# Attention normalised in its transposed layout, with its sums sent over DRAM, rotary partners swapped by DMA, and a new table of positions

## The reference

```python
xn = _layernorm(x)
x = x + _L0_attn_ref(xn, ...) + _L0_ffn_ref(xn, ...)
# plain attention: 16 heads of 8 channels
attn = exp_x / (sum(exp_x) + 1e-6)          # exp_x = exp(clip(scores - max, -50, 50))
out = (attn @ v) @ Wout.T
# second block: the same attention with rotary q and k
r = [x1 * cos - x2 * sin, x1 * sin + x2 * cos]   # neighbours x1, x2 of a head
x = rmsnorm(src + softmax(q k / sqrt(8)) v Wo)
shared = swiglu(x @ W_shared_in) @ W_shared_out
routed = sum over 8 experts of (h @ W2[e]) * w[:, e]   # two experts of a row have w > 0
out = rmsnorm(x + shared + routed)
```

## Time and profile before

| what | value |
|---|---|
| median of three runs | 2111.24 us (2108.23 to 2111.75) |
| the profiled execution | 2110.22 us, span 2108.4 us |
| mean granted TensorE clock | 0.993 |
| busy: PE, DVE, ACT, POOL | 1957.9, 1629.0, 1442.8, 1135.9 us |
| DMA: moved, mean rate | 81.93 MB, 39 GB/s |

### The profile page before, as it was taken

The page is one execution under the profiler, slowest core; times in us unless marked ns, Lnnn a source line. Parts: engine busy times, 40 slices in busy tenths (PEclk is TensorE's granted clock), DMA queues, the critical chain, the costliest instruction groups (busy, mean ns, idle before and its releaser), DMA issues.

```text
span 2108.4 us, 43905 instructions
## 1 busy us (share of the span) xinstructions
PE 1957.9 (93%) x10694; PEld 602.4 (29%) x10694; DVE 1629.0 (77%) x2948; ACT 1442.8 (68%) x2993; POOL 1135.9 (54%) x1695
## 2 busy tenths in 40 slices
PE   4998899999999999999999999999999999999885
PEld 1222223232332323233232323323232222323232
DVE  3878897878879787887978788797978879797421
ACT  0367677777777777777777777777777777777752
POOL 1352637456473746647374664737466473746434
PEclk9999999999999999999999999999999999999997
DMA  2101010101101010110101010010101001010000
GB/s 92 43 27 50 28 53 31 56 27 53 36 24 56 29 57 26 52 36 25 56 28 58 26 55 32 26 56 27 59 26 54 31 27 56 26 56 18 22 0 16
DMA packets 79167, 81.93 MB, mean 39 GB/s; under 512 B 14716, under 2 KB 66172, under 8 KB 78844
## 3 DMA queue, kind: packets, MB, share of 16 engines
q1 hardware_dynamic: 78984, 80.20, 11.2%
HBM read 11.36 MB, written 4.19 MB: 7 GB/s over the span
## 4 chain that ended last, share of the span: by engine, by line
PE 71%; DVE 12%; issue 7%; ACT 6%; POOL 2%; SPq 1%; DVEq 1%; ACTq 0%; DMA 0%; POOLq 0%
PE o_ps L501 19%; PE score_ps L467 19%; PE side_ps L580 10%; DVE negmax L757 7%; PE side_ps L567 6%; PE shift_ps L482 5%; PE side_ps L549 5%; PE side_ps L516 3%; ACT weights L614 3%; DVE x L785 2%; PE side_ps L553 2%; PE side_ps L538 2%; PE side_ps L572 1%; ACT spread L649 1%; DVE stats L846 1%
## 5 line engine op out<-in xcount | busy, mean ns | idle before, releaser
L757 DVE TENSOR_REDUCE negmax<-score_ps 128x1 f32<-128x512 f32 x2048 | 1308.4, 682 | 350.0 <-PE score_ps L467 326.4
L614 ACT ACTIVATE weights<-shift_ps 128x512 f32<-128x512 f32 x2048 | 1161.2, 599 | 517.9 <-PE shift_ps L482 491.1
L482 PE MATMUL shift_ps<-qt,kt 51*128 51x512 bf16 x2048 | 691.3, 387 | 46.7 <-ACT weights L614 42.3
L467 PE MATMUL score_ps<-kt,qt 48*128 48x512 bf16 x2048 | 658.1, 393 | 58.6 <-DVE negmax L757 32.3
L954 POOL TENSOR_SCALAR weights<-weights 128x2048 f32<-128x2048 f32 x256 | 485.1, 1895 | 138.5 <-ACT weights L614 109.8
L501 PE MATMUL o_ps<-weights,vt 128*32 128x512 f32 x4096 | 550.1, 610 | 0.3 <-POOL weights L954 0.3
L467 PEld LDWEIGHTS score_ps<-kt,qt 48*128 48x128 bf16 x2048 | 131.7, 94 | 683.7 <-DVE negmax L757 544.6
L580 PE MATMUL side_ps<-w_sb,hidden 128*128 128x512 f32 x512 | 252.2, 617 | 9.9 <-ACT spread L649 8.1
L482 PEld LDWEIGHTS shift_ps<-qt,kt 51*128 51x128 bf16 x2048 | 150.4, 93 | 220.7 <-ACT weights L614 210.5
L649 ACT ACTIVATE spread<-side_ps,gate 128x128 f32<-128x128 f32 x512 | 159.8, 377 | 26.3 <-PE side_ps L580 26.3
L567 PE MATMUL side_ps<-x1T,w_up_sb 128*128 128x512 f32 x256 | 148.2, 665 | 6.3 <-DVE hidden L817 4.7
(11 more groups left out here) (111 smaller groups left out, 1452.0 us busy)
## 6 DMA issues: line engine op xcount, KB each, us to landing
qt<-q_parts SPq DMA_DIRECT2D x768, 32.0 KB
kt<-k_parts SPq DMA_DIRECT2D x768, 32.0 KB
x_in<-in_x_dram SPq DMA_DIRECT2D x16, 256.0 KB, 2.7
xn_mid<-xn_new SPq DMA_DIRECT2D x16, 256.0 KB, 2.4
xn_old<-xn_mid SPq DMA_DIRECT2D x16, 256.0 KB, 2.4
res_new<-in_x_dram SPq DMA_DIRECT2D x16, 256.0 KB, 2.6
res_old<-res_new SPq DMA_DIRECT2D x16, 256.0 KB, 2.7
out_dram<-out_sb SPq DMA_DIRECT2D x16, 256.0 KB, 2.6
```

The lines of the kernel that those rows point to most:

```text
L467: pe.matmul(score_ps[:, score_bank(a, t), :], qt[a][row:row + HROWS, slot, 128 * tile:128 * tile + 128], kt[a][row:row + HROWS, slot, :], ...
L482: pe.matmul(shift_ps[:, t % 2, :], kt[a][row:row + HROWS + MROWS, slot, 128 * tile:128 * tile + 128], qt[a][row:row + HROWS + MROWS, slot, ...
L614: act.activation(weights[:, i % 8, tile, :], shift_ps[:, t % 2, :], ACT.Exp, scale=SCALE).then_inc(weighed, 1)
L757: dve.tensor_reduce(negmax[:, i // 8, tile, i % 8:i % 8 + 1], score_ps[:, score_bank(a, t), :], AX.X, ALU.max, negate=True).then_inc(max_t ...
```

## The change

- **Normalisation in the transposed layout.** The jobs `o_*` and `back_*`, `normalise` and the copies into `headsT` go. `copy_o` still copies `o_ps` into `o_sb`; SP stores `o_sb` (256 KB) in DRAM (`move_o`), waits for it, and reads back the sums as `den` [128, 2, 32] and the channels as `heads_raw`. VectorE inverts `den` (`invert`, quarter 27 of each half); SP stores the inverses and, after that landed, reads them back repeated over the eight channels (`widen`) as `inv_wide`; GpSimd multiplies (`divide`) into `headsT`. `y_*` waits for that and stands at quarter 41 instead of 31.
- **Rotary partners by DMA.** `qs_rope` and `ks_rope` go. Channels are reordered on the chip so that partners lie 64 partitions apart (six ScalarE copies of the weights at the start). VectorE makes both products from one bank, two DMAs swap the halves of the sin product (`swing`), GpSimd adds it (`turn`). `q_rope` and `k_rope` move into the odd half before. cos and sin are loaded in four broadcast DMAs. `place_qk` reads every fourth partition instead of 32 neighbours.
- **Clips.** Every fourth head's clip goes from GpSimd to VectorE, as two instructions of 128x1024 with the lower bound alone; GpSimd keeps twelve.
- **Tables.** VALUE_AT is 3 instead of 1; all positions in EVEN and ODD are new (shared_out moves to the even half); banks are emptied one to two quarters later than before; the four row-tile pieces of the scalings, statistics and normalisation on VectorE, which stood together, are one per quarter or per two quarters.

The core of the diff; the remaining lines are the new positions on ScalarE and VectorE, semaphores and tiles:

```diff
+VALUE_AT = 3
...
+EVEN = [("v0", [1]), ("x1T", [3]), ("v1", [5]), ("gates", [9]), ("max_rope1", [11]), ("up0", [13]), ("down0", [17]),
+        ("up1", [21]), ("down1", [25]), ("up2", [29]), ("down2", [33]), ("up3", [37]), ("y_plain", [41]),
+        ("max_plain0", [43]), ("down3", [45]), ("shared_out", [53])]
+ODD = [("xnT", [1]), ("q_plain", [5]), ("max_plain1", [7]), ("k_plain", [9]), ("exp0", [13]),
+       ("exp1", [17]), ("exp2", [21]), ("exp3", [25]), ("exp4", [29]), ("exp5", [33]), ("exp6", [37]), ("y_rope", [41]),
+       ("max_rope0", [43]), ("exp7", [45]), ("q_rope", [53]), ("k_rope", [57])]
...
+AT = {"merge": 40, "invert": 27, "hi0": 7, "hi1": 9, "mid0": 13, "mid1": 17, "copy1": 21, "copy0": 53, "z": 33, "shares": 34, "top": 28,
+      "square_x1": 46, "scale_x1": 55, "square_out": 6, "scale_out": 13, "stats": 44, "moments": 51, "norm": 59}
...
                         sp.dma_start(kt[a][row:row + 8, 4 * gh:4 * gh + 4, :],
-                                     k_parts[a][p:p + 32, K_PART[t], :]).then_inc(qk_landed[a][gh], 16)
+                                     k_parts[a][c:128:4, K_PART[t], :]).then_inc(qk_landed[a][gh], 16)
 
             def place_max(b, job):
...
+            def move_o(b, job):
+
+                lag, a, gh = O_LAG[job], int(job[2:-1] == "rope"), int(job[-1])
+                if live(b, lag):
+                    hold(o_copied, cnt(b, lag, 4, 2 * a + gh + 1))
+                    if gh == 0:
+                        hold(normed, cnt(b, lag, 2, a))
+                    hold(den_moved, cnt(b, lag, 64, 16 * (2 * a + gh)))
+                    hold(rows_moved, cnt(b, lag, 64, 16 * (2 * a + gh)))
+                    sp.dma_start(o_rows, o_sb[:]).then_inc(o_out, 16)
+                    hold(o_out, cnt(b, lag, 64, 16 * (2 * a + gh + 1)))
+                    by_head = o_rows.rearrange("(r c) n -> r c n", c=16)
+                    sp.dma_start(den[:, gh, :], by_head[:, DH, :].rearrange("r (p n) -> r p n", n=DEN)).then_inc(den_moved, 16)
+                    sp.dma_start(heads_raw[64 * gh:64 * gh + 64, :], by_head[:, 0:DH, :]).then_inc(rows_moved, 16)
+
+            def widen(b, a):
+
+                if live(b, -1):
+                    hold(inv_done, cnt(b, -1, 2, a + 1))
+                    hold(inv_back, cnt(b, -1, 32, 16 * a))
+                    sp.dma_start(inv_rows.rearrange("(g h) (p n) -> (h p) g n", g=2, n=DEN), inv_den[:])\
+                        .then_inc(inv_out, 16)
+                    hold(inv_out, cnt(b, -1, 32, 16 * (a + 1)))
+                    hold(normed, cnt(b, -1, 2, a))
+                    sp.dma_start(inv_wide[:], inv_rows.unsqueeze(1).broadcast_to([H, DH, S]))\
+                        .then_inc(inv_back, 16)
+
+            def swing(b, n):
+
+                if live(b, 1):
+                    taken(sp, b, ("q_rope", "k_rope")[n])
+                    stand(sp)
+                    hold(rope_done, cnt(b, 1, 2, 0))
+                    for d0 in range(2):
+                        sp.dma_start(swung[64 * d0:64 * d0 + 64, n, :],
+                                     turned[64 * (1 - d0):64 * (1 - d0) + 64, n, :]).then_inc(swung_landed[n], 16)
...
                 place_max(b, "max_rope1")
+                move_o(b, "o_plain1")
...
+                widen(b, PLAIN)
                 place_qk(b, 0, ROPE, 0)
                 place_max(b, "max_plain0")
+                move_o(b, "o_rope0")
 
             def odd(b):
                 place_qk(b, 0, ROPE, 1)
                 place_max(b, "max_plain1")
+                move_o(b, "o_rope1")
+                widen(b, ROPE)
                 place_qk(b, 1, PLAIN, 0)
                 place_max(b, "max_rope0")
+                move_o(b, "o_plain0")
+                swing(b, 0)
+                swing(b, 1)
...
-                        pe.wait_ge(clip_pool, cnt(b, lag, H, 4 * quad + 4))
+                        pe.wait_ge(clip_pool, cnt(b, lag, 12, 3 * quad + 3))
+                        pe.wait_ge(clip_dve, cnt(b, lag, 8, 2 * quad + 2))
...
-                            if t == after("odd", f"exp{n}", 1 + half):
+                            if t == after("odd", f"exp{n}", 2 + 2 * half):
...
+            def clip(b, i, part):
+
+                if live(b, 0):
+                    dve.wait_ge(weighed, cnt(b, 0, 2 * UNIT, NT * i + 2 * part + 2))
+                    half = weights[:, i % 8, 2 * part:2 * part + 2]
+                    dve.tensor_scalar(half, half, FLOOR, None, ALU.max).then_inc(clip_dve, 1)
+
+            def invert(b, a):
+
+                if live(b, -1):
+                    dve.wait_ge(den_moved, cnt(b, -1, 64, 32 * (a + 1)))
+                    need(dve, inv_out, cnt(b, -1, 32, 16 * a))
+                    if a == PLAIN:
+                        dve.tensor_scalar(den[:], den[:], EPS_DEN, None, ALU.add).then_inc(den_done, 1)
+                        dve.wait_ge(den_done, cnt(b, -1, 1, 1))
+                    dve.reciprocal(inv_den[:], den[:]).then_inc(inv_done, 1)
...
+                    if (t - AT["scale_x1"]) % 2 == 0:
+                        scale(b, x1, x1, 0, -1, x1_done, (t - AT["scale_x1"]) // 2)
+                    for n, job in enumerate(("q_rope", "k_rope")):
+                        if t == after("odd", job) and live(b, 1):
+                            full(dve, b, job)
+                            need(dve, rope_rest, cnt(b, 1, 2, 0))
+                            need(dve, swung_landed[n], cnt(b, 1, 32, 0))
+                            dve.tensor_tensor(roped[:, n, :], bank(job), cos, ALU.mult)
+                            dve.tensor_tensor(turned[:, n, :], bank(job), sin, ALU.mult).then_inc(free(job), 1)
+
...
+            def turn(b, n):
 
                 if live(b, 0):
-                    taken(pool, b, ("q_rope", "k_rope")[n])
-                    taken(pool, b, last)
-                    pool.tensor_tensor(roped[:, n, :], roped[:, n, :], turned[:, :], ALU.add).then_inc(rope_done, 1)
+                    pool.wait_ge(swung_landed[n], cnt(b, 0, 32, 32))
+                    stand(pool)
+                    pool.tensor_tensor(roped[:, n, :], roped[:, n, :], swung[:, n, :], ALU.add).then_inc(rope_done, 1)
+
+            def divide(b, a):
+
+                if live(b, -1):
+                    pool.wait_ge(inv_back, cnt(b, -1, 32, 16 * (a + 1)))
+                    pool.wait_ge(rows_moved, cnt(b, -1, 64, 32 * (a + 1)))
+                    y = (b + (-1), "y_rope") if a == PLAIN else (b, "y_plain")
+                    if live(y[0], LAG[y[1]]):
+                        full(pool, *y)
+                    pool.tensor_tensor(headsT[:, :], heads_raw[:, :], inv_wide[:, :], ALU.mult).then_inc(normed, 1)
...
             def even(b):
-                clip(b + (-1), 15)
+                turn(b, 0)
+                turn(b, 1)
...
-                split_max(b, "max_plain0")
                 if live(b, -2):
                     router(b, True)
+                divide(b, PLAIN)
+                split_max(b, "max_plain0")
                 if live(b, 1):
```

More of the change, by code:

```diff
@@ L243, in layer_kernel @@
         ones_made = sem("ones_made")
+        wq_made = sem("wq_made")
         kt_ones = sem("kt_ones")
@@ L599, in step @@
                         side(b, job)
-            all_steps(pe, lambda b: step(b, "even"), lambda b: step(b, "odd"), merge_weights)
+            all_steps(pe, lambda b: step(b, "even"), lambda b: step(b, "odd"))
         @block.scalar
@@ L677, in even @@
                         copy_side(b, "x1T", x1T[:, :])
[L678 removed]
+                    if t == after("even", "max_rope1", 2):
                         copy_max(b, "max_rope1")
[L680 to L681 removed]
+                    part(b, 0, t, "q_rope", AT["hi0"], ROPE, roped[:, 0, :], q_parts, True)
+                    part(b, 0, t, "k_rope", AT["hi1"], ROPE, roped[:, 1, :], k_parts, True)
                     for n in range(4):
[L683 removed]
+                        if t == after("even", f"up{n}", 3) and live(b, -2):
                             full(act, b, f"up{n}")
@@ L804, in even @@
                                           ALU.add).then_inc(free("gates"), 1)
-                    for job, dst, table in (("q_rope", roped[:, 0, :], cos), ("qs_rope", turned[:, :], sin),
-                                            ("k_rope", roped[:, 1, :], cos), ("ks_rope", turned[:, :], sin)):
-                        if t == after("even", job) and live(b, 0):
-                            full(dve, b, job)
-                            need(dve, rope_rest, cnt(b, 0, 2, 0))
-                            if job == "ks_rope":
-                                dve.wait_ge(rope_done, cnt(b, 0, 2, 1))
-                            dve.tensor_tensor(dst, bank(job), table, ALU.mult).then_inc(free(job), 1)
                     for n in range(4):
-                        if t == after("even", f"up{n}", 2) and live(b, -2):
+                        if t == after("even", f"up{n}", 3) and live(b, -2):
                             dve.wait_ge(tanh_done, cnt(b, -2, 4, n + 1))
```

(13 more changed lines are left out.)

257 lines of the change are left out of this document (123 added, 134 removed), and 3 rows, old and new, of the table EVEN.

## The result

The changed kernel takes 2204.04 us (median of 4, 2193.28 to 2205.54) against 2110.26 (median of 4) for the kernel before beside it: 1.0434 times the time, 95% interval 1.0404 to 1.0464. I had forecast 2068 and a range of 2012 to 2138: wrong in sign and outside the range. The profiled execution of the changed kernel took 2193.28 us, its span is 2191.5, so 83.1 us longer than the span before.

The account below looks back on a forecast made before the run. PE and DVE together were taken to hold the even half, PE the odd. 57.5 + 62.0 = 119.5 against 122.6 a batch, over fifteen steps -45, last batch +2: 2110.2 to 2067, 2068 by the median; range 2012 to 2138.

Parts of the forecast that it names:

- the wait at y_plain: Even half, quarter 41: headsT comes 2.9 us after PE is ready; no fall of TensorE's clock priced behind it.
- the chain of flights: Even half, SP's queue: o's store, moves, inverses out and back, then GpSimd's product; headsT ready at 907.0.
- o's copy: Even half: ACT copies o at quarter 21, at 0.82 us a quarter about 888, starting the way over DRAM.
- Rival 2: Even half: y_plain's wait grows 1.8 us and halves TensorE's clock, +3; batch 124.3, total 2138 us; chance 0.22.
- the turn: Odd quarters 49 to 64, into the even half: 16.0 us of DVE work against 11 of PE, then 1.2 given back.
- three scalings: Odd quarters 49 to 64, on DVE: three x1 scalings at their median 0.61, 1.8 us together.
- odd quarters 0 to 13: Start of the odd half, without shared_out: 10.8 us, scaled from today's 16.1 us for 17 quarters.
- quarters 13 to 49 of the odd half: Stretch with all eight experts, y and a max: 36.4 us, with DVE's clips, inversion and additions fitting beside it.
- DVE's wait of 2 us for den: Even half, quarter 27: DVE reaches invert at 890.6, den lands at 893.2, so DVE stands 2 us or so.
- The tail: Last batch: the way over DRAM has only experts beside it; +2 us taken (0 to 12).
- The even half without the stall: Forecast for the even half: 57.5 us, ending at about 925.9, with the wait of 2.9 in it.
- rival 1: Whole loop: PE's full saving of 6.5 us per batch arrives, y_plain finds headsT ready; 2014 us; chance 0.18.

Follow-up runs that it names:

- e2_rope: Against the changed kernel: q_rope and k_rope at odd quarters 13 and 15 instead of 53 and 57, exp0 to exp7 one slot later; 2187.75 us.
- e4_fill: Against the changed kernel: PE multiplies three unused 128x512 f32 blocks ahead of y_plain's wait for headsT in the even half; 2171.34 us.
- e1_widen: Against the changed kernel: SP's even half issues inv_rows and inv_wide right behind xn_old's move, ahead of the other moves; 2129.92 us.
- f3_all: Against the changed kernel: earlier inverses, q_rope/k_rope, max_rope1 splitting, y_rope divide and q_plain parts; DVE's hidden product one quarter later; 2065.15 us.

## Why the prediction was wrong

**The step that failed** is the wait at y_plain: "Against it: I work out a wait of 2.9, for which no row shows a fall". The place, its cause in SP's queue and the chain of flights were right: 2.05 + 2.94 + 5.12 + 2.19 + 3.01 + 1.26 us were measured where I had 2.6, 2.63, 5.13, 2.6, 2.6 and 1.26 (2.94 and 5.12 from issue to issue, as 2.63 and 5.13 were). One term agrees by luck: o's copy "at quarter 21" would be at 868.4 + 21 x 0.82 = 885.6 and not 888, but the half starts slower than that pace, and the store left 19.4 us into it, close to what I wrote. The wait was 3.40 in the batch shown and 3.8 in the mean. The size hardly matters, because the clock also fell behind waits of 2.96 and, in e2_rope, 2.67: the wait of 2.9 that I worked out would have been no defence. One fall behind 4.71 shows that such a wait is enough; it says nothing of shorter ones, and I priced the clock behind mine at nothing. e4_fill prices it at 33 us and e1_widen the whole place at 74. Rival 2, which I gave 0.22 and let begin at 4.7, is what happened in the even half; its 2138 is still 66 short, and it holds nothing of the turn.

**The second step that failed** is the turn: "Fifteen maxima 9.3, two clips 2.4, four rotary products 2.5, three scalings at their median 0.61 1.8: 16.0", and then 1.2 given back. Quarters 49 to 64 took 18.6, of which 1.2 is DVE's wait at the jump, and the even half starts 2.0 later on top. The two clips there were cheaper than I had them (1.9 and not 2.4). The scalings are the term that was mis-sized: four of them stand there, at quarters 55, 57, 59 and 61, and not three, and they took 4.3 in the mean of eleven batches against my 1.8. Two of the four end right behind GpSimd's clips: 1.27 and 1.63 us in the turn shown, where a scaling takes 1.01 in the mean of all 64. The 1.2 that I gave back did not come. The groups after (xcount | busy us, mean ns | idle before):

```profile
L834 DVE TENSOR_SCALAR weights<-weights 128x1024 f32<-128x1024 f32 x128 | 99.8, 781 | 0.0
L856 DVE SCALAR_TENSOR_TENSOR x<-x,rms,norm_sb 128x128 f32<-128x128 f32 x64 | 64.2, 1007 | 1.6 <-POOL rms L1021 1.6
```

I took the median of a quantity whose long values belong to just this place, and priced DVE as a sum where the clock falls beside it as well; what that fall costs no run shows.

**What I did not look at:** the tables also move tanh and hidden into one quarter. DVE stood 0.46 us in front of each of four products, in a stretch where DVE had become the bound. And k_plain waits for the bank that q_plain's rest frees, 19.7 us in the whole kernel, 1.2 a batch, which is most of why odd quarters 0 to 13 take 12.3 and not 10.8 (11.3 in f3_all, where the first parts of q_plain come sooner). Its row on the page after:

```profile
L615 PE MATMUL side_ps<-xnT,wq_sb 128*128 128x512 f32 x96 | 58.7, 696 | 21.1 <-DVE q_rest L940 19.7
```

**What held:** quarters 13 to 49 of the odd half at 36.4 (36.2). q and k issues at 0.72 despite partitions in steps of four (0.65). The reciprocal with its addition at 0.9 (0.73). DVE's wait of 2 us for den did not come: den landed before quarter 27. The tail was 9 us shorter, not 2 longer. The even half without the stall, 57.6 in e1_widen, looks like the 57.5 that I wrote with a wait of 2.9 in it, but that agreement is luck: mine was cut some 2 us earlier, as the earlier trace rows is, and tanh and the turn fill the place of the wait. With the waits found here removed, f3_all's batch is 120.7, 2.1 below before: rival 1's 6.5 is not reached there, and the half clock at the turn remains.

## What to carry to other kernels

A wait of the leading engine has two prices, its length and the clock behind it: two small edits that remove 3.8 us and 1.8 us of waiting a batch were worth 74 and 20 us here, and a filler of useless products in the first of the two waits was worth 33. At the turn, where PE had no such wait, fillers lost time. In an in-order queue, ask of each transfer that waits for a landing who stands behind it; moving one call past two landings gave back most of the loss. When work is moved onto an engine near a loop's turn, count that stretch quarter by quarter with the durations of that stretch, not with medians over the kernel.

## What the runs showed of the hardware

TensorE's granted clock fell to 0.50, its 1.2 GHz level, behind each of the fifteen waits at y_plain, 2.96 to 4.79 us, behind one of 2.67 in e2_rope, and also at the turn behind waits of 0.60 and 1.33 us close together, with 3.73 of 5.73 us busy ahead of the fall. The Trainium skill, TensorE: Matmul & The Clock Gate, section The HAM clock gate, ties the level to how busy the array has been of late; the turn agrees, where no single wait is long. Two scalings that ran beside GpSimd clips in the turn shown took 1.27 and 1.63 us and ended 0.15 and 0.14 us behind the end of a clip. A DVE clip of 128x1024 f32 in place took 0.68 us undisturbed (min/median/max below), as long as a 128x512 product of two inputs; the estimate of 0.7 that the prediction worked out from the Trainium skill, VectorE: DVE Perf Modes, section The perf-mode tier table, was right and my 1.2 was not.

```profile
L834 DVE TENSOR_SCALAR weights<-weights x128: 677/684/2307, 97.5 to 2062.4; 128x1024 f32<-128x1024 f32 x128
```

A store of 32 KB to DRAM landed in 1.7 us in the median, the 256 KB spread back over the heads in 3.3 (columns as in the earlier trace rows):

```profile
inv_wide<-inv_rows SPq DMA_DIRECT2D x32, 256.0 KB, 3.3
...
inv_rows<-inv_den SPq DMA_DIRECT2D x32, 32.0 KB, 1.7
```
